# Key scores of the next head pair: from two steps of attention with half each to four steps with a quarter each

## The reference, cut to what matters

```python
def _softmax_kernel(x, proj, is_query):
    dd = jnp.einsum('bhnd,md->bhnm', x * data_norm, proj)
    diag = 0.5 * jnp.sum(x * x, axis=-1) * data_norm ** 2
    stab = jnp.max(dd, axis=-1) if is_query else jnp.max(dd, axis=(-1, -2))
    return ratio * (jnp.exp(dd - diag[..., None] - stab) + EPS_K)

def _linear_attention(qp, kp, v):
    d_inv = 1.0 / jnp.einsum('bhnm,bhm->bhn', qp, kp.sum(axis=2))
    ctx = jnp.einsum('bhnm,bhnd->bhmd', kp, v)
    return jnp.einsum('bhnm,bhmd,bhn->bhnd', qp, ctx, d_inv)
```

## Time and profile before

| what | value |
|---|---|
| time, median of 3 runs (lowest, highest) | 1312.62 us (1310.42, 1312.62) |
| the profiled execution's own time | 1312.36 us |
| its span, first to last instruction | 1310.5 us |
| PE, DVE, ACT, POOL busy | 1182.3, 835.2, 316.5, 309.0 us |
| attention of layer 0, layer 1 | about 133 to 250 us, 560 to 680 us |

### The profile page before, as it was taken

One profiled execution on the slowest core, in us unless ns is written; L12 is line 12 of the kernel. 1 busy time (PEld: TensorE's weight loads), 2 busy tenths in 40 slices (PEclk: granted clock), 3 DMA queues, 4 the chain that ended last, 5 costly groups with the idle time before them and its releaser, 6 DMA issues.

```text
span 1310.5 us, 16673 instructions
## 1 busy us (share of the span) xinstructions
PE 1182.3 (90%) x5960; PEld 924.6 (71%) x5960; DVE 835.2 (64%) x1705; ACT 316.5 (24%) x592; POOL 309.0 (24%) x221
## 2 busy tenths in 40 slices
PE   4788899999999989888999999997888999899695
PEld 3666799888788867678898878883444688787432
DVE  6577777689744457777767974426777217418756
ACT  4245435222001015534422211100111111011212
POOL 4240202019422420020200942420000415100316
PEclk8889989999999989999999999998999999999787
DMA  5300101004201200010100321332000011001001
GB/s 200 152 10 1 33 2 33 1 1 129 65 33 33 93 1 1 1 33 1 34 1 1 113 67 46 119 118 65 0 1 1 9 34 58 8 1 31 1 0 65
DMA packets 15931, 52.12 MB, mean 40 GB/s; under 512 B 2641, under 2 KB 3473, under 8 KB 15217
## 3 DMA queue, kind: packets, MB, share of 16 engines
q1 hardware_dynamic: 12208, 40.23, 9.3%
q10 hardware_dynamic: 3648, 10.86, 2.3%
HBM read 44.80 MB, written 6.29 MB: 39 GB/s over the span
## 4 chain that ended last, share of the span: by engine, by line
PE 57%; DVE 23%; issue 15%; ACT 3%; POOL 2%; DMA 0%; POOLq 0%; DVEq 0%; ACTq 0%
PE ps_a L420 6%; PE ps_v L420 6%; PE ps_a L422 6%; PE ps_a L421 6%; PE ps_v L421 6%; PE ps_v L422 6%; PE ps_a L677 4%; PE ps_v L577 4%; DVE f_hi L1193 4%; PE ps_v L590 3%; PE ps_v L781 2%; DVE f_lo L1195 2%; DVE qmax L1366 2%; PE ps_v L441 2%; PE ps_a L441 2%
## 5 line engine op out<-in xcount | busy, mean ns | idle before, releaser
L420 PE MATMUL ps_a<-ht_hi,w_hi 128*128 128x512 f32 x496 | 196.5, 396 | 9.6 <-DVE headmask_r L1278 7.2
L422 PE MATMUL ps_a<-ht_hi,w_lo 128*128 128x512 f32 x496 | 195.3, 394 | 0.0
L421 PE MATMUL ps_a<-ht_lo,w_hi 128*128 128x512 f32 x496 | 195.2, 393 | 0.0
L1007 POOL TENSOR_TENSOR w_lo<-stage,w_hi 128x1024 fp32r<-128x1024 f32 x58 | 148.3, 2556 | 32.8 <-issue 28.5
L806 ACT ACTIVATE work<-ps_a,col_sb 128x512 f32<-128x512 f32 x96 | 66.7, 719 | 321.5 <-PE ps_a L422 207.7
L1005 POOL CAST w_hi<-stage 128x1024 fp32r<-128x1024 f32 x58 | 67.0, 1155 | 261.5 <-PE ps_a L422 160.6
L420 PEld LDWEIGHTS ps_a<-ht_hi,w_hi 128*128 128x128 f32 x496 | 94.5, 191 | 32.5 <-DVE headmask_r L1278 7.6
L1396 DVE TENSOR_TENSOR xm<-ps_v,xm 128x512 f32<-128x512 f32 x80 | 55.2, 691 | 94.3 <-PE ps_v L422 93.8
L420 PE MATMUL ps_v<-w_hi,ht_hi 128*128 128x512 f32 x224 | 93.0, 415 | 17.8 <-issue 10.3
L422 PEld LDWEIGHTS ps_a<-ht_hi,w_lo 128*128 128x128 f32 x496 | 94.3, 190 | 20.2
L421 PEld LDWEIGHTS ps_a<-ht_lo,w_hi 128*128 128x128 f32 x496 | 94.3, 190 | 19.7
(11 more groups left out here) (198 smaller groups left out, 2178.6 us busy)
## 6 DMA issues: line engine op xcount, KB each, us to landing
stage<-wstream SPq DMA_DIRECT2D x62, 512.0 KB, 3.5
xt_d<-xt_hi SPq DMA_DIRECT2D x2, 1024.0 KB, 5.0
xt_d<-xt_lo SPq DMA_DIRECT2D x1, 2048.0 KB, 11.4
ht_hi<-xt_d ACTq DMA_DIRECT2D x1, 2048.0 KB, 9.3
ht_lo<-xt_d ACTq DMA_DIRECT2D x1, 2048.0 KB, 15.1
x_again<-x ACTq DMA_DIRECT2D x8, 256.0 KB, 4.3
out<-xm SPq DMA_DIRECT2D x8, 256.0 KB, 2.0
rows_sb<-rows ACTq DMA_DIRECT2D x2, 768.0 KB, 4.6
```

The lines of the kernel that those rows point to most:

```text
L420: nc.tensor.matmul(ps, left[0], right[0], start=first, stop=False)
L421: nc.tensor.matmul(ps, left[0], right[1], start=False, stop=False)
L422: return nc.tensor.matmul(ps, left[1], right[0], start=False, stop=last)
L1007: nc.gpsimd.tensor_tensor(lo, stage[:, j, :], hi.bitcast(f32), ALU.subtract).then_inc(w_split, 1)
```

## The change

A pair's key scores now come in four steps, two pieces (one token group, both heads) in each, and the first quarter comes one step earlier than before: ahead of step 0 for pair 1, in step 3 for pair 2, in step 7 for pair 3. Steps -1 to 2 hold pair 1, steps 3 to 6 pair 2, steps 7 to 10 pair 3. The last quarter falls into step s = 2, ahead of ctx. `k_bias` moves from s = 2 to s = 3, and the exponentials of the keys on ACT move one step later, to s = 3, 0 and 1. The numbers of instructions of each kind stay as they were.

```diff
--- before.py
+++ after.py
@@ -71,11 +71,12 @@
 def attention_order():
 
 
+    yield "ddk", -1
     for g in range(STEPS + 2):
         pair, s = divmod(g, NT // 2)
         if g < STEPS:
             yield "ddq", g
-            if s < 2 and pair + 1 < NH // 2:
+            if g + 1 < STEPS - NT // 2:
                 yield "ddk", g
         if s == 2 and g < STEPS:
             yield "ctx", pair
@@ -90,8 +91,8 @@
 
 
 def ddk_ahead(g):
-    pair, s = divmod(g, NT // 2)
-    return pair + 1, range(2 * s, 2 * s + 2)
+    pair, s = divmod(g + 1, NT // 2)
+    return pair + 1, range(s, s + 1)
 
 
 def ring_v_attention():
@@ -893,9 +894,9 @@
                                                         psA[:, i % BANKS, M * n:M * (n + 1)], ACT.Exp, scale=DN,
                                                         bias=qbias[:, g % 4, j, n:n + 1])
                         last.then_inc(a_empty, 1)
-                        part_ = 2 * ((s + 2) % 4) + j
-                        if part_ < 6 and NT // 2 <= g + 2 <= STEPS + 1 and g + 2 < 4 * (NH // 2):
-                            exp_k((g + 2) // 4, (2 * NT * part_ + 5) // 6, (2 * NT * (part_ + 1) + 5) // 6)
+                        part_ = 2 * ((s + 1) % 4) + j
+                        if part_ < 6 and NT // 2 <= g + 1 < STEPS:
+                            exp_k((g + 1) // 4, (2 * NT * part_ + 5) // 6, (2 * NT * (part_ + 1) + 5) // 6)
                 for h in range(H):
                     for k in range(KT):
                         i = MIX_A[("o", h, k)]
@@ -1381,7 +1382,7 @@
                             nc.vector.tensor_tensor(V[:, 2 * s:2 * s + 2, pair, 1 + DH * j:1 + DH * (j + 1)], ps[:, :, 1 - j:1 - j + DH],
                                                     rden[:, g % 2, j, :].unsqueeze(2).to_broadcast([P, 2, DH]),
                                                     ALU.mult).then_inc(v_empty, 1)
-                    if what == "ddq" and s == 2 and pair + 1 < NH // 2:
+                    if what == "ddq" and s == 3 and pair + 1 < NH // 2:
                         k_bias(pair + 1)
                     if what == "at" and g < NT:
                         nc.vector.tensor_tensor(Xm[:, g, :], Xm[:, g, :], rows_sb[:, 2, :], ALU.add)
```

## The result

| what | before | after |
|---|---|---|
| time, median of 4 runs (lowest, highest) | 1311.57 us (1310.42, 1312.62) | 1335.22 us (1330.44, 1338.15) |
| ratio after / before, 95% interval | | 1.0177 (1.0145 to 1.0209) |
| the profiled execution: own time, span | 1312.36, 1310.5 us | 1330.44, 1328.5 us |

The change made the kernel slower by 1.8%. The sign was forecast, but the time lies above the range of 1312 to 1328; the profiled execution, the fastest of the four, does too. It is 18.1 us over that of before, where 11.5 were forecast. The three executions without a profile took 4.3 to 7.7 us more than the profiled one, at a mean granted clock of 0.950 to 0.952 instead of 0.959.

What follows compares the result with a forecast made beforehand. DVE was taken to set the pace except while PE computes a context. Starts -2.96, four periods 4 x 1.32, `k_bias` 2 x 0.57 and collisions 2 x 4.0 gave +11.5 us on 1312.36: 1323.9 us, range 1312 to 1328.

Steps and rivals of the forecast that it cites:

- The sign: Whole kernel: the change makes it slower, chance 0.80 of a slowdown over 0.2%.
- The bubble: Steps with key scores: at waits four ring places behind a piece, stalling DVE's tr copies; 1.03 us, newly opening in s = 3.
- a period: Context to context in attention: 0.94 + 2.82 - 2.44 = +1.32 us, four of them in all.
- pieces in s = 2: Step s = 2: eight matmuls ahead of the context cost PE +0.94 us; DVE's work there costs nothing.
- `k_bias` in step 11: Step 11 gets pair 3's `k_bias`, which PE feels through ACT: +0.57 us in each layer.
- Rival 3: Steps with two pieces: the bubble does not open, a period is -1.77 us, 1303.4 us without a collision; chance 0.07.
- The collision: Step 11: POOL's weight splits hold DVE's L1369 1.4 us, then 0.3 us, and `k_bias` 2.3 us; 4.0 us a layer.
- rival 1: Step 11: POOL and DVE miss each other, or only L1369 blocks; 0 or 1.7 us, 1315.8 to 1319.3; chance 0.22.
- the clock is entered at nothing: PE's clock: no cost in the sum, both signs left to the range, despite new PE gaps.
- Rival 2: Step 12, both layers: the clock falls in PE's gap, 1.26 us each, 1326.4; some 1330 if reaching contexts; chance 0.13.
- The start: Up to context 0: it begins earlier, -0.85 us in layer 0 and -2.11 in layer 1, together -2.96 us.
- it meets the L1369 that takes 1.25 us at the same time as before: Start of layer 0: DVE reaches the held L1369 unchanged, so context 0 starts at 143.97 instead of 144.82.

Runs made afterwards that it cites:

- e4: Kernel before with its first key-score group moved to step s = 3 and none in s = 2: 1318.53 us, ratio 1.0045.
- e3: Changed kernel with no key scores in step s = 3 and two of the four groups in s = 0: 1327.83 us, ratio 1.0122.
- e1: Changed kernel with POOL's split of the weight behind pair 3 delayed to the last query scores: 1319.36 us, ratio 1.0061.
- e2: Changed kernel with twelve unused matmuls on PE ahead of the transposes in steps 1, 3 to 5 and 7 to 9: 1327.66 us, ratio 1.0125.
- e7: Changed kernel with both POOL's delayed weight split and the twelve unused matmuls on PE: 1315.42 us, ratio 1.0024.
- late split: Edit: POOL asks for the weight behind pair 3 only at the last query scores; on the changed kernel 1319.36 us, ratio 1.0061.
- e5: Kernel before with the key scores of steps s = 0 and 1 placed behind at within the step: 1311.03 us, ratio 1.0007.
- e8: Kernel before with key scores behind at in the step and POOL's weight split delayed: 1310.55 us, ratio 0.9994.
- e12: Kernel before with key scores behind at, POOL's weight split delayed and five unused matmuls on PE: 1306.71 us, ratio 0.9964.
- e11: Kernel before with POOL's weight split delayed and eight unused matmuls ahead of the transposes: 1314.95 us, ratio 1.0026.

## Why the prediction was right, and where it failed

**The sign and the mechanisms of order held.** The bubble opens in three steps of a period: in the changed kernel DVE waits 0.66 us ahead of the first tr copy in steps s = 3, 0 and 1 (162.06, 168.53 and 174.99). At full clock a period costs 1.40 us more (32.62 against 31.22), where I had +1.32, and its parts were measured alone: a bubble 1.02 (e4; I had 1.03), pieces in s = 2 with `k_bias` 0.35 (e3). `k_bias` in step 11 costs 0.54 (e1; 0.57). Rival 3, no bubble with two pieces, is out by e4.

**The collision was found at its place, and its direct price was too high.** It held DVE 2.35 us in layer 0 and 2.45 in layer 1 of the changed kernel, 3.2 and 3.4 where the period before it ran at full clock (e2), against 4.0. The instruction in doubt was `k_bias`, with one tensor in SBUF. It lasts 2.48 us, so rival 1 with 1.7 us is out; its condition that L1369 be 1.5 us late was all but met, and the price fell on `k_bias` alone. The Trainium skill ("SBUF — State Buffer", section "Who interferes with whom") makes the shared port pair of DVE and GpSimd an exclusive lock in which the loser fully blocks; the ends at 228.88 and 228.72 agree. The same section frees an operation with one SBUF input only outside the two-port modes, and counts tensor_scalar among those that can enter one. So it does not free L1332, as the prediction thought it might, and the 2.48 us fit it; in which mode the instruction ran no row here shows.

**The step that failed is "the clock is entered at nothing".** I had seen the lower clock in the earlier trace rows and listed the new gaps, and still let the price be zero with both signs. The runs show three places. In the second period of each layer it costs 1.7 us (34.33 against 32.58 in e2, where the gaps are filled). Behind the collision, the stretch to context 3 lost 6.8 us, of which 0.54 are `k_bias` and 2.35 the held DVE; the other 3.9 us in layer 0, and as much in layer 1, are what is left by subtraction, and lie beside PE at 1.2 GHz (granted 0.63, 0.50 and 0.59 from 228 to 240). And context 0 of layer 0 lost 1.65 us at the lower clock. Together that is 2 x 1.7 + 2 x 3.9 + 1.65 = 12.9 us where the sum had nothing. Rival 2 was the right one in kind and place, but I priced it at 1.26 us a layer, from a fall with 1.7 us of missing clock (568 to 576 in layer 1 of before); the one behind the collision has 5.1 us of it. It had 0.13. That its high end, 1330, is the profiled execution's time is luck: it was for a fall that reaches into whole contexts, and context 3 ran at full clock; and it held 8.0 us for the held DVE, which took 4.8, and 3.0 us gained at the start, which were not.

**The start was mis-signed in layer 0**, +2.31 against -0.85, and near in layer 1, -2.17 against -2.11. The step "it meets the L1369 that takes 1.25 us at the same time as before" took the position of POOL's split as fixed. It moved by 1.0 us against DVE, and the clock fell behind the longer gap. In e1 and e7, with the same order there, the start takes 19.31 and 19.36 us, 0.4 less than before; so this part belongs to the execution as much as to the order. In layer 1 the hit is in part luck too: in e1, with the same list up to there, the clock fell (0.73 and 0.84 from 572 to 580), and the start took 21.21 us, 0.5 less than before.

**The sum in hindsight**, profiled execution, with the forecast behind it: starts +0.1 (-3.0), four periods +8.1 (+5.3), last stretches +13.65 (+9.1), of these `k_bias` 1.1 (1.1), the held DVE 4.8 (8.0) and the clock 7.8 (0); the rest of the program -3.8 (0); in all 18.1. On medians, the change without collision and clock costs 3.65 us (e7) of 23.65. The late split alone takes the ratio from 1.0177 to 1.0061; so about two thirds of the loss is the collision and what it did to the clock.

**Open.** Why the clock falls behind some gaps and not others: in the first period of layer 0, the stretch of 164 to 168 has PE busy for 2.54 us, as in the one ahead of the fall at 208, and the next one is at 1.00; and e5 and e8 differ at the same gap of 1.45 us. The second periods of the changed order fell in all four cases without a fill ahead of them and with `k_bias` in its place (after, e1) and in none of four with it (e2, e7); more than that the traces don't tell. The unprofiled runs of the changed kernel have a lower mean clock than the profiled one, but no trace shows where. In e12 the last 0.3 to 0.9 us of a period over e5's 29.72 were not looked into; the five matmuls are a possible share of them.

## What to carry to other kernels

Spreading work evenly over steps pays only if what stalls is proportional to the work; here the stall was a fixed 1.03 us for each step that had any, because a consumer stands four places behind it in a ring, so the same work in fewer steps, or behind the consumer, is better. Before moving a producer, look at what its engine does next: a later all-reduce pushed POOL's weight splits onto DVE's shortest instructions on the path. And if PE has gaps, price the clock over the work that follows the gap, and test with matmuls that nobody reads, put where the gap comes after them.

## What the runs showed of the chip that I had not expected

- The clock can undo a gain in full. Key scores last shortened a period to 29.7 us (three of four in e5), and with a gap of 1.46 us and the granted share at 0.70 it was 31.1 to 31.2 again (all four in e8, and one in e5).
- Matmuls that nobody reads can make a kernel faster: twelve of them, 1.58 us, took 1.7 us off the second period of a layer (e2), while eight of them behind the gap instead of ahead of it cost some 1.5 us a period (e11).
- Two DVE instructions on 128x8 numbers, each with one tensor from SBUF and a scalar for each partition, take 0.37 us together alone and 2.48 us beside POOL's TENSOR_TENSOR. The one on 128x2 numbers just before them (L1329, 0.16 us, from 226.21) came between a CAST, over at 226.27, and that TENSOR_TENSOR, begun at 226.35, and was not held.
- Between the first CAST behind an all-reduce and its TENSOR_TENSOR, POOL stands 6.7 to 7.9 us in the rows shown, and at the same place, with the same list of instructions up to it, 7.87 us in after and 6.78 in e1. A schedule that must miss a split by less than that is not safe.
